# Attention in a twelve-stage decoder: new homes for the score banks, masks ahead of the queries, key copies behind the norms

## The reference, cut to what matters

```
L0x, L1a, L3a: causal;   L1x: plus a bias -slope * |i - j|;   L2x: a padding mask
scores[b,h] = Q[b,h] @ K[b,h].T (+ bias or mask);   P = softmax(scores * scale)
y = concat_heads(P @ V) @ Wo (+ bo);   x = x + y
```

## Time and profile before

| | us |
|---|---|
| median of 3 runs (lowest, highest) | 783.21 (782.43, 784.71) |
| the profiled execution | 782.54 |
| its span in the trace | 780.8 |
| mean granted PE clock over the span | 0.877 |
| PE, DVE, ACT, POOL busy | 604.5, 497.1, 243.5, 118.6 |
| line 1155, row maxima, 80 instructions | 98.0 |
| line 1161, subtraction, 80 instructions | 97.7 |
| line 1245, normed x, 96 instructions | 34.1 busy by form |
| line 333, key copies on POOL, 34 instructions | 37.5 |

### The profile page before, as it was taken

How to read it: one execution, slowest core, us unless ns; L and a number is a source line. 1 busy time by engine, 2 the same in 40 slices (tenths; PEclk the granted TensorE clock), 3 DMA queues, 4 the chain that set the end, 5 groups by cost and what they waited for, 6 DMA issues and landing times.

```text
span 780.8 us, 10935 instructions
## 1 busy us (share of the span) xinstructions
PE 604.5 (77%) x4305; PEld 393.9 (50%) x4305; DVE 497.1 (64%) x1338; ACT 243.5 (31%) x357; POOL 118.6 (15%) x118
## 2 busy tenths in 40 slices
PE   1306299977899789987997577899779968997376
PEld 1305145567455536665775545455535653565335
DVE  7777877667487647655244645786564355775694
ACT  0423124414244313333423331244221122343150
POOL 5021611014210212001002014110200043102110
PEclk9957579979899959997998798999789987999778
DMA  9600000000000000000000000000000000000000
GB/s 313 262 0 1 0 1 2 2 1 2 0 2 1 2 1 1 2 1 1 0 1 1 1 0 1 1 2 1 1 0 1 0 1 1 1 2 0 1 0 28
DMA packets 6722, 12.42 MB, mean 16 GB/s; under 512 B 528, under 2 KB 4880, under 8 KB 6288
## 3 DMA queue, kind: packets, MB, share of 16 engines
q1 hardware_dynamic: 6672, 11.73, 4.2%
HBM read 11.21 MB, written 0.52 MB: 15 GB/s over the span
## 4 chain that ended last, share of the span: by engine, by line
PE 68%; DVE 23%; ACT 4%; POOL 3%; issue 2%; DMA 1%; POOLq 0%; DVEq 0%; SPq 0%; ACTq 0%
PE ps L404 51%; PE ps L469 10%; PE ps L487 3%; DVE xn L1245 3%; PE ps L426 3%; DVE st L1077 2%; POOL rs L322 2%; DVE mx L1155 1%; DVE big L1161 1%; DVE x L1175 1%; DVE mv L1080 1%; DVE big L1087 1%; ACT td L823 1%; ACT big L843 1%; PE ps L676 1%
## 5 line engine op out<-in xcount | busy, mean ns | idle before, releaser
L1155 DVE TENSOR_REDUCE mx<-ps 128x8 f32<-128x1024 f32 x80 | 98.0, 1225 | 66.9 <-PE ps L404 66.8
L843 ACT ACTIVATE big<-ps 128x1024 f32<-128x1024 f32 x80 | 81.9, 1024 | 145.7 <-PE ps L469 145.7
L1161 DVE TENSOR_TENSOR big<-ps,mx 128x1024 f32<-128x1024 f32 x80 | 97.7, 1222 | 4.7 <-DVE mx L1155 0.5
L404 PE MATMUL ps<-KTm,qk 32*128 32x512 f32 x320 | 96.5, 680 | 0.0
L322 POOL TENSOR_TENSOR rs<-ve,negh 128x4 f32<-128x4 f32 x26 | 26.6, 1024 | 420.6 <-DVE ve L1082 420.5
L469 PE MATMUL ps<-kt,big 128*128 128x128 f32 x640 | 88.4, 283 | 2.3 <-DVE big L1161 2.0
L404 PE MATMUL ps<-xnT,wt 128*128 128x512 f32 (+1 forms) x148 | 84.1, 711 | 3.1 <-DVE big L1400 3.1
L469 PEld LDWEIGHTS ps<-kt,big 128*128 128x128 f32 x640 | 71.9, 144 | 23.5 <-DVE big L1161 12.5
L404 PE MATMUL ps<-wt,big 128*128 128x128 f32 (+1 forms) x480 | 61.0, 280 | 0.0
L404 PEld LDWEIGHTS ps<-wt,big 128*128 128x128 f32 (+1 forms) x480 | 56.4, 191 | 8.0 <-issue 6.0
L333 POOL TENSOR_TENSOR KTm<-qk,kt 128x512 f32<-128x512 f32 x34 | 37.5, 1111 | 117.4 <-PE ps L404 108.9
(11 more groups left out here) (252 smaller groups left out, 797.5 us busy)
## 6 DMA issues: line engine op xcount, KB each, us to landing
wt<-in_weights SPq DMA_DIRECT2D x1, 1664.0 KB, 17.8
wt<-in_weights SPq DMA_DIRECT2D x1, 1603.0 KB, 12.5
wt<-in_weights SPq DMA_DIRECT2D x6, 256.0 KB, 11.7
bt<-in_bconsts SPq DMA_DIRECT2D x1, 1024.0 KB, 8.9
rowt<-in_rows SPq DMA_DIRECT2D x1, 975.0 KB, 5.9
wt<-in_weights SPq DMA_DIRECT2D x1, 832.0 KB, 14.1
wt<-in_weights SPq DMA_DIRECT2D x1, 608.0 KB, 19.2
wt<-in_weights SPq DMA_DIRECT2D x1, 580.0 KB, 5.8
```

The lines of the kernel that those rows point to most:

```text
L404: return pe.matmul(out, lhsT, rhs, start=start, stop=stop, **k)
L843: act.activation(half, heads_of(pair(g, u)), ACT.Exp, scale=SCALES[l]).then_inc(*s.step(f"exp{u}"))
L1155: dve.tensor_reduce(top, S, AX.X, ALU.max).then_inc(*s.step())
L1161: dve.tensor_tensor(pr[:, half * HH:(half + 1) * HH, :].rearrange("p (i j) k -> p i j k", i=2), S, top.unsqueeze(3).to_broadcast([P, 2, HG ...
```

## The change

It has five parts. (1) The pairs become banks (1, 2), (5, 6), (3, 4), and the value banks 0 and 7. Group 0's first unit then uses its own key and value banks, group 1's first unit its own; the pair (3, 4) of the third unit is group 0's bank 3 and group 1's bank 0. (2) The loop's opening wait asks for the own group only; group 0's second unit waits for the queries of group 1. (3) The masks of a unit are a function of their own, `masked`. In L1x and L2x the masks of unit 0 stand at phase 3, behind a wait for the own keys and values and ahead of the query projection; in L0x, L1a and L3a they stand at phase 20. (4) POOL's first key copies in L1x and L2x wait for `xn` of both groups, and the second one of a group goes to phase 2. (5) The value bias of L1x and L2x is one DVE instruction of 128 x 512 for each group in place of four of 128 x 128. The output projection turns into bank 0 (group 1: bank 7), projects into bank 3 (group 1: bank 4), and waits for the own group alone.

```diff
@@ -174,7 +174,8 @@
         return bank
 
     all_banks = ps[:, :].rearrange("p (b c) -> p b c", c=512)
-    PAIRS = (all_banks[:, 4:6, :], all_banks[:, 2:4, :], all_banks[:, 0:2, :])
+    PAIRS = (all_banks[:, 1:3, :], all_banks[:, 5:7, :], all_banks[:, 3:5, :])
+    VALUES = tuple(all_banks[:, k, :] for k in (0, 7))
 
     def pair(g, u):
 
@@ -325,9 +326,12 @@
 
                 first = 0 if l in ("L1x", "L2x") else 1
                 for b in range(first, GB):
-                    yield n, ((1 if first == 0 else 19) if b < 2 else beat(g, 2 * b - 4, 3))
+                    yield n, ((1 + b if first == 0 else 19) if b < 2 else beat(g, 2 * b - 4, 3))
                     if b == first:
                         pool.wait_ge(*s.at(f"{l}.KT"))
+                        if first == 0:
+                            for other in range(GROUPS):
+                                pool.wait_ge(*s.at(f"{l}.xn", other))
                     if b >= 2:
                         pool.wait_ge(*s.at(f"{l}.S{2 * b - 3}"))
                     pool.tensor_tensor(t.KTm[:, b % 2, :, :], keys_of(t, b), own_head(), ALU.mult).then_inc(*s.step(f"keys{b}"))
@@ -450,12 +454,16 @@
                         mask = t.dmask[:, u // 2, :] if l == "L2x" else causalb
                         mm(out, identb, mask.unsqueeze(1).to_broadcast([P, HG, P]), stop=False)
 
+                def masked(u):
+                    if 2 * u + g >= 3:
+                        pe.wait_ge(*s.at(f"{l}.exp{(2 * u + g - 3) // 2}", 1 - g))
+                    elif u:
+                        pe.wait_ge(*s.at(f"{l}.QT", 1))
+                    for i in range(2):
+                        biased(u, i)
+
                 def scores(u):
                     b, half = divmod(u, 2)
-                    if 2 * u + g >= 3:
-                        pe.wait_ge(*s.at(f"{l}.exp{(2 * u + g - 3) // 2}", 1 - g))
-                    for i in range(2):
-                        biased(u, i)
                     if half == 0:
                         pe.wait_ge(*s.at(f"{l}.keys{b}"))
                     for i in range(2):
@@ -477,25 +485,29 @@
                     pe.wait_ge(*s.at(f"{l}.exp{u}"))
                     for j in range(HH):
                         h, at = HH * half + j, 32 * (j % HG)
-                        ins = mm(all_banks[at:at + 32, 6 + g, h // HG * P:(h // HG + 1) * P], t.vaug[:, b, h, :], PT[:, (u % 2) * HH + j, :], tile_position=(0, at))
+                        ins = mm(VALUES[g][at:at + 32, h // HG * P:(h // HG + 1) * P], t.vaug[:, b, h, :], PT[:, (u % 2) * HH + j, :], tile_position=(0, at))
                     ins.then_inc(*s.step(f"O{u}"))
 
                 def back(b):
 
                     pe.wait_ge(*s.at(f"{l}.OT{b}"))
                     for i in range(GB):
-                        ins = pe.transpose(all_banks[:, 6 + g, i * P:(i + 1) * P], t.td[:, i, :], ident)
+                        ins = pe.transpose(VALUES[g][:, i * P:(i + 1) * P], t.td[:, i, :], ident)
                     ins.then_inc(*s.step(f"OR{b}"))
 
-                yield n, 20
-                for other in (g, 1 - g):
-                    pe.wait_ge(*s.at(f"{l}.QT", other))
-                    pe.wait_ge(*s.at(f"{l}.KT", other))
-                    pe.wait_ge(*s.at(f"{l}.vaug", other))
+                pe.wait_ge(*s.at(f"{l}.KT"))
+                pe.wait_ge(*s.at(f"{l}.vaug"))
                 if l == "L1x":
                     pe.wait_ge(loaded["alibi"], 16)
                 if l == "L2x":
                     pe.wait_ge(*s.at("L0a.dmask"))
+                masked(0)
+                if l in ("L1x", "L2x"):
+                    yield n, 4
+                    pe.wait_ge(*s.at(f"{l}.xnT"))
+                    project_cols(0, xnT, w(f"{l}_wq"), "q")
+                yield n, 20
+                pe.wait_ge(*s.at(f"{l}.QT"))
                 scores(0)
                 for u in range(UNITS):
                     yield n, beat(g, u, 2)
@@ -503,6 +515,7 @@
                         back(u // 2 - 1)
                     turned(u)
                     if u + 1 < UNITS:
+                        masked(u + 1)
                         scores(u + 1)
                     if u:
                         weighted(u - 1)
@@ -511,15 +524,13 @@
                 yield n, beat(g, UNITS, 2)
                 back(GB - 1)
 
-            def out_proj(n, l, weight, turn=2, out=0):
+            def out_proj(n, l, weight):
                 yield n, 130
-                if l in SCALES:
-                    pe.wait_ge(*(s.at(f"{l}.exp{UNITS - 2}", 1) if g == 0 else s.at(f"{l}.co{GB - 1}", 0)))
                 pe.wait_ge(*s.at(f"{l}.co{GB - 1}"))
-                turn_rows(turn, t.co, "coTp")
+                turn_rows(3 * g, t.co, "coTp")
                 yield n, 131
                 pe.wait_ge(*s.at(f"{l}.coT"))
-                project_rows(out, t.coT, weight, "y")
+                project_rows(3 - 3 * g, t.coT, weight, "y")
 
             def gates(bk, weight, n):
                 for b in range(GB):
@@ -598,15 +609,19 @@
                     turn_rows(0, t.tc, "QTp")
                     pe.wait_ge(*s.at(f"{l}.krot"))
                     turn_rows(1, t.td, "KTp")
+                    yield n, 20
                     yield from attend(n, l)
                     yield from out_proj(n, l, w(f"{l}_wo"))
+                if l == "L1a":
+                    yield n, 4
+                    pe.wait_ge(*s.at("L1a.xnT"))
+                    project_cols(0, xnT, w("L1a_wq"), "q")
+                    project_cols(1, xnT, w("L1a_wk"), "k")
+                    project_rows(2, xnT, w("L1a_wv"), "v")
+                    yield n, 20
+                if l in ("L1x", "L2x"):
+                    yield n, 3
                 if l in ("L1a", "L1x", "L2x"):
-                    yield n, 4
-                    pe.wait_ge(*s.at(f"{l}.xnT"))
-                    project_cols(0, xnT, w(f"{l}_wq"), "q")
-                    if l == "L1a":
-                        project_cols(1, xnT, w("L1a_wk"), "k")
-                        project_rows(2, xnT, w("L1a_wv"), "v")
                     yield from attend(n, l)
                     yield from out_proj(n, l, w(f"{l}_wo"))
                 if l == "L0f":
@@ -847,12 +862,12 @@
                 yield n, beat(g, UNITS, 1)
                 weighted_out(GB - 1, l)
                 yield n, 130
-                read(t.coT[:, :], bank(2), "coTp", "coT")
+                read(t.coT[:, :], bank(3 * g), "coTp", "coT")
 
             def weighted_out(b, l):
                 if b:
                     act.wait_ge(*s.at(f"{l}.OR{b - 1}"))
-                read(t.td[:, :, :], four(all_banks[:, 6 + g, :]), f"O{2 * b + 1}", f"OT{b}")
+                read(t.td[:, :, :], four(VALUES[g]), f"O{2 * b + 1}", f"OT{b}")
 
             for n, l in enumerate(LAYERS[1:STAGES + 1]):
                 s.begin(l)
@@ -1131,7 +1146,7 @@
             def attend(n, l):
                 def normal(b):
                     dve.wait_ge(*s.at(f"{l}.OR{b}"))
-                    O = all_banks[:, 6 + g, :].rearrange("p (h d) -> p h d", h=H)
+                    O = VALUES[g].rearrange("p (h d) -> p h d", h=H)
                     dve.reciprocal(t.rc[:, :], O[:, :, HD]).then_inc(*s.step())
                     dve.wait_ge(*s.last())
                     dve.tensor_tensor(t.co[:, b, :].rearrange("p (h d) -> p h d", h=H), O[:, :, 0:HD],
@@ -1144,9 +1159,9 @@
                 if l in ("L1x", "L2x"):
                     yield n, 3
                     dve.wait_ge(*s.at(f"{l}.v"))
-                    for b in range(GB):
-                        dve.tensor_tensor(t.vaug[:, b, :, 0:HD], bank(2)[:, b * P:(b + 1) * P].rearrange("p (h d) -> p h d", h=H),
-                                          row(f"{l}_bv").rearrange("p (h d) -> p h d", h=H), ALU.add).then_inc(*s.step("vaug"))
+                    dve.tensor_tensor(t.vaug[:, :, :, 0:HD], bank(2).rearrange("p (b h d) -> p b h d", b=GB, h=H),
+                                      row(f"{l}_bv").rearrange("p (h d) -> p h d", h=H).unsqueeze(1).to_broadcast([P, GB, H, HD]), ALU.add)\
+                       .then_inc(*s.step("vaug"))
                 for u in range(UNITS):
                     yield n, beat(g, u, 1)
                     half = u % 2
@@ -1336,7 +1351,7 @@
                     rotate(bank(0).rearrange("p (h d) -> p h d", d=HD), const("c3"), const("s3"), tc, "qrot", "pair")
                 if l in ("L0x", "L1a", "L1x", "L2x", "L3a"):
                     yield from attend(n, l)
-                    yield from add(n, l, 0)
+                    yield from add(n, l, 3 - 3 * g)
                 if l == "L0f":
                     yield from top2(n, l, E0, "bg0")
                     yield from mix(n, l, range(1, E0, 2), [e % 3 for e in range(E0)], lambda e: 21 + 4 * e)
```

## The result

The changed kernel took 765.0 us (median of 4, 763.26 to 765.44) against 783.86 for the kernel before in the same comparison; the ratio is 0.9757, 95% interval 0.9734 to 0.9780. The forecast was 766.6, its range 762 to 776. The total was right, and partly by luck: its parts were near in three stages (L1a, L1x, L3a) and off by 2 us or more in three others (L0x, L2x and L2f), whose errors cancelled.

What follows compares the result with a forecast made beforehand. PE bounds the kernel, its loops full, so gains lie in the five attention heads and PE's clock there. 0.9 + 0.8 + 9.0 + 5.0 + 0.9 = 16.6 us off 783.2 gives 766.6, range 762 to 776.

Steps and rivals of the forecast that it cites:

- Part 1: L1x, L2x heads: key copies behind both norms bring group 1's turn 2.9 us earlier; late copies cost nothing.
- Part 2: L1x, L2x: one value add for four takes 0.7 us, between bounds of 0.6 and 1.23.
- Part 3, L1x: L1x head: with masks ahead of queries and full clock, second transposes come at 283.65 instead of 292.66; gain 9.0 us.
- rival A: L1x, L2x heads: the clock falls all the same, gains only 3.4 and 1.9; both: 775.3 us; chance 0.27.
- the stretch with 2.06 us of work: Earlier profile: the clock was said to stay full in it, against a fall in one with 1.64.
- Part 3, L2x: L2x head: row maxima at 486.35 instead of 491.36, full clock from there on; gain 5.0 us.
- Part 3, the masks' place: L1x, L2x: masks ahead of queries win little, costing PE 1 us before the queries and returning it behind them.
- Part 4: Own banks and waits start masks earlier: 0.8 us in L1a, 0.9 each in L0x and L3a, 0 at the loop's end.
- Rival D: L1x, L2x norms are slow for another reason than the copies; only the layout's 2.6 remain, 780.6 us; chance 0.06.
- B: L1x, L2x: key copies hold the value adds as they held the norms; 783 to 784.5 us; chance 0.07.
- C: Attention loops: new pairs lengthen each of 80 units; slower, 790.6 us at 0.3 a unit; chance 0.06.

Runs made afterwards that it cites:

- e1: Kernel before with one edit: POOL's first key copies in L1x and L2x wait for xn of both groups, second copies go to phase 2; 769.65 us, ratio 0.9817.
- e3: Kernel before plus 14 unused matmuls on PE behind the turn of group 0's xn in L1x and L2x; 773.43 us, ratio 0.9864.
- e5: Changed kernel plus 7 unused matmuls behind group 1's first scores in L1a, L1x and L2x; 762.27 us, ratio 0.9703.
- e4: Changed kernel with the first masks of L1x and L2x back behind the query projection; 763.31 us, ratio 0.9726.
- e8: Changed kernel run again, unedited, for the spread of its stages; 764.0 us, ratio 0.9749.
- e9: Kernel before plus three unused matmuls behind group 1's query projection in L1x; 778.76 us, ratio 0.9939.
- e2: Changed kernel with the key copies of L1x and L2x put back beside the layer norm; 773.24 us, ratio 0.9861.
- e7: Kernel before with the new banks and own waits alone; 770.79 us, ratio 0.9827.
- e6: As e5, plus unused matmuls in PE's idle stretches in the heads of L0f, L1f, L2f, L3a and L0x; 749.71 us, ratio 0.9570.

## Why the prediction was right, and where it was not

- *Part 1, copies behind the norms*: as predicted. The turn came 2.93 earlier relative to the first xn (2.9 forecast), and e1 shows that nobody waits for the late copies. That the value adds don't collide is shown too: 686 ns each beside the copies, and an add of the same shape with POOL idle (`add`, 465.23) takes 0.69. This is what the Trainium skill ("SBUF — State Buffer", "Who interferes with whom") says of an instruction with at most one SBUF input; a tensor_scalar is one that it says can contend with GpSimd, and e1 against the kernel before measures the norm's: 2.36 us or 5.29 for the eight.
- *Part 2*: 686 ns each, 0.7 forecast. Not tried alone.
- *Part 3, L1x*: 9.0 forecast, 9.8 by stage. The clock held, rival A was wrong for this stage, and the split between waiting and clock is e3's. The reading of the earlier trace rows that stood behind it was wrong: the stretch with 2.06 us of work was not at full clock throughout (its column says 0.92). The clock came back at 731.6, 0.60 of that work lies before, and from there to 735.0 PE worked 1.46 of 3.40 us. So that row said nothing of a margin; that the clock would hold was a guess that came true in L1x.
- *Part 3, L2x*: 5.0 forecast, 2.5 measured. The first transposes did come 5.5 earlier relative to the first xn (9.6 instead of 15.1). The step that failed is "It was at full clock from there on, so the rest moves with it": the clock fell at 479.0, and 3.1 us went back. The prediction says that "no gap is above 0.6 us after the first turn". Its own sum has one: in L1x group 1's scores, 1.06 behind group 0's 278.1, end at about 279.2, and the first transposes come at 280.7. The gap measured is 1.73 in both stages. I had looked for gaps ahead of the queries and not behind the scores, though both groups' scores now end before the first subtraction. e5 shows that filling this gap keeps the clock in L2x. Rival A's price for L2x, a gain of 1.9, was nearer, though the clock fell in the loop and not in the head.
- *Part 3, the masks' place*: "wins little", and e4's total agrees.
- *Part 4*: 0.8 in L1a and 0.9 in L3a against 1.4 and 1.0 by stage; in L0x the wait of 0.9 is gone, but the clock came back at 110.4 and not at 107.0 as in the one profile of before, and the stage was 1.1 longer. In e8 it was 1.6 shorter than before. The 0.9 that the sum has for L0x is neither shown nor refuted by these two.
- *Not in the sum*: L2f, 3.5 shorter, in both traces of the changed kernel. The instructions are the same; in the kernel before the clock fell a second time within the stage, in the changed one it did not. Stretch of the kernel before:

```profile
571.20:578.00 6.80, 6.12 (x7) 2.52 (x8) 3.79 (x14) 1.19 (x2) 0.00 (x0) 0.50 0.00 0
```

  In the traces without fillers in this stage, L2f's length goes with this second fall alone: 76.5 or 76.6 where it lasts 6.8 us (before, e1, e9), 75.1 where it lasts 3.4 (e2, e4, e7), 72.8 to 73.1 where there is none (changed, e8, e3, e5). It does not go with the change: e3 has none of the change and no second fall, e4 has nearly all of it and one. So the gain is real in the traces, but it isn't the layout's or the copies'; what decides on the fall is open. The errors, 2.5 too much in L2x, 2.0 too much in L0x and 3.5 too little in L2f, cancelled, with 0.8 from L1x and 0.6 from L1a.
- *Rival D's price*: "only the layout's 2.6 remain" was wrong by 10. The layout alone gave a ratio of 0.9827. I counted each wait at its length; e9 shows that the 1.04 us in L1x was worth 4.3. Some 3.4 of these 10 lie in L2f, L1f and L2a, where no edit of e7 explains them. Copies alone 1.8%, layout alone 1.7%, together 2.4%; in L1x 9.5, 3.9 and together 9.8 us: both act on the same stretch of PE's work, and the second pays less.
- *Rivals B and C*: B is refuted by the value adds' durations, C by the unchanged pitch of the units (3.09 us in L1a, 2.95 in L1x, before and after).

## What to carry to other kernels

Price an idle stretch of TensorE by what the clock does behind it, not by its length, and look for all of them in a head, also the ones that the change opens. Cut the trace into stages before a gain is put down to an edit: here stages that no edit touched moved by up to 3.7 us. GpSimd's work on SBUF beside VectorE's SBUF-to-SBUF norm more than doubled the norm's time; behind the norm it cost nothing here, since its result is wanted later. If a wait can't be removed, unused matmuls in it may pay: here 14 us on top of the change (764.0 in e8 to 749.7 in e6).

## What the runs showed of the hardware

TensorE's clock can stay low while the engine has no idle time. In L0x of the changed kernel it was at 1.2 GHz for 14.3 us in which PE was busy throughout, with masks, scores and transposes; in L1x of the kernel before, PE was busy 6.80 of 6.80 us from 281.1 to 287.9, and the clock came back at 291.3. It can also fall with little idle time before. In e6 the fillers had bridged the wait in L0f's head until 160.8; then came the two turns, with at most 0.59 us between them, and 64 gate matmuls of 8 columns (162.77 to 171.77), and the clock fell at 164.8 in the midst of them. Stretches of the changed kernel (first line) and of e6:

```profile
96.00:110.30 14.30, 14.30 (x40) 6.10 (x40) 8.04 (x7) 2.65 (x3) 3.22 (x3) 0.50 0.00 0
...
161.00:165.00 4.00, 3.38 (x27) 3.15 (x28) 2.29 (x9) 1.42 (x3) 0.07 (x1) 0.97 0.00 0
...
165.20:168.50 3.30, 3.30 (x19) 3.30 (x19) 3.10 (x18) 0.00 (x0) 0.00 (x0) 0.55 0.00 0
```

The fillers did help the clock here: it was low for 3.4 us in e6, against 10.2 in the kernel before. The last of the gate matmuls ended 13.0 us behind the start of POOL's first root of L0f (158.78), against 15.7 in the kernel before, so PE gained 2.7. Yet the stage is only 1.2 shorter: the rest is lost behind them, where the stage doesn't hang on PE alone. So a low clock isn't worth the same in every stage.

The spread between executions of one kernel, 5.5 us in e4 and 5.6 in e5, goes with the mean granted clock (0.885 or 0.889 against 0.916 or 0.918), in one core's runs on one chip.
